# Cross-attention with a bit-weight feed-forward: the attention outputs leave in groups of eight heads instead of four

## The reference, cut to what matters

```python
x = x + xattn(layernorm(x), ctx, ctx)   # causal, softmax(q k^T / 8) v for each head
x = x + (layernorm(x) @ weight.T + bias)
# weight[o, i] = scale * sum_n (sigmoid(pweight) - sigmoid(nweight))[o, i, n] * exps[n] * sigmoid(mask)[n]
# bias[o] = rounded(clip(sum_n (pbias - nbias)[o, n] * bexps[n])) * biasscale
```

## Time and profile before

| | |
|---|---|
| median of 3 runs | 1179.91 us (1177.99 to 1181.48) |
| profiled execution, its own time | 1179.6 us |
| its span | 1177.8 us |
| mean granted TensorE clock | 0.987 |
| PE busy | 1099.1 us, 93% |
| DVE busy | 996.0 us, 85% |
| ACT busy | 855.9 us, 73% |
| POOL busy | 493.5 us, 42% |

### The profile page before, as it was taken

One profiled execution on the slowest core, in us unless ns is written; L12 is line 12 of the kernel. 1 busy time (PEld: TensorE's weight loads), 2 busy tenths in 40 slices (PEclk: granted clock), 3 DMA queues, 4 the chain that ended last, 5 costly groups with the idle time before them and its releaser, 6 DMA issues.

```text
span 1177.8 us, 32049 instructions
## 1 busy us (share of the span) xinstructions
PE 1099.1 (93%) x13092; PEld 809.3 (69%) x13092; DVE 996.0 (85%) x1558; ACT 855.9 (73%) x1764; POOL 493.5 (42%) x510
## 2 busy tenths in 40 slices
PE   4788988999999999999999999999999998999988
PEld 3677755676676777777776777777776676777753
DVE  5766788999988888999989888999989888998961
ACT  6789766778786677777876777878776777777740
POOL 3444424344236654343335655333335664331150
PEclk8899999999999999999999999999999999999989
DMA  9999726675669876656778886676678976664442
GB/s 320 321 322 351 242 73 138 148 160 113 140 121 202 200 169 143 141 140 135 134 132 201 195 162 134 133 153 140 116 149 202 189 169 121 133 119 86 89 84 72
DMA packets 382594, 191.13 MB, mean 162 GB/s; under 512 B 358128, under 2 KB 358128, under 8 KB 378352
## 3 DMA queue, kind: packets, MB, share of 16 engines
q1 hardware_dynamic: 381440, 189.05, 69.9%
q10 hardware_dynamic: 1008, 0.04, 0.1%
HBM read 67.15 MB, written 16.78 MB: 71 GB/s over the span
## 4 chain that ended last, share of the span: by engine, by line
PE 49%; DVE 19%; ACT 13%; DMA 8%; issue 6%; POOL 3%; SPq 2%; ACTq 0%; POOLq 0%; DVEq 0%
PE ffnb L473 16%; PE ptb L434 8%; PE slot L420 5%; PE slot L421 5%; DMA pd<-pd 5%; DVE pd L661 4%; DVE mx L647 4%; ACT p L542 4%; PE obank L454 4%; ACT pd L551 3%; ACT pt L558 3%; PE ffnb L497 3%; PE obank L457 3%; PE obank L455 3%; DVE stats L679 3%
## 5 line engine op out<-in xcount | busy, mean ns | idle before, releaser
L542 ACT ACTIVATE p<-slot,mx 128x512 f32<-128x512 f32 (+7 forms) x512 | 377.0, 744 | 137.2 <-issue 74.3
L647 DVE TENSOR_REDUCE mx<-slot 128x1 f32<-128x640 f32 (+7 forms) x352 | 356.1, 1014 | 31.7 <-PE slot L424 30.8
L473 PE MATMUL ffnb<-wt,yt 128*128 128x512 f16 x1464 | 372.4, 381 | 1.1 <-DMA yt<-y 0.8
L653 DVE SCALAR_TENSOR_TENSOR pt<-ptb,pt 128x512 f16<-128x512 f32 (+1 forms) x504 | 281.6, 598 | 51.4 <-ACT pt L558 49.9
L558 ACT ACTIVATE pt<-ptb 128x512 f16<-128x512 f32 (+1 forms) x504 | 239.8, 526 | 106.1 <-PE ptb L434 105.3
L420 PE MATMUL slot<-kt,qt 128*128 128x128 f16 (+3 forms) x1056 | 267.6, 283 | 7.1 <-DMA qs<-qt 2.5
L421 PE MATMUL slot<-kt,qs 128*128 128x128 f16 (+3 forms) x1056 | 267.6, 283 | 0.0
L883 POOL TENSOR_TENSOR ring<-ring,att 128x256 f32<-128x256 f32 x128 | 93.1, 727 | 393.1 <-DVE att L672 392.9
L434 PE MATMUL ptb<-id,p 128*128 128x128 f32 x1700 | 238.1, 278 | 10.8 <-DVE pt L653 10.6
L473 PEld LDWEIGHTS ffnb<-wt,yt 128*128 128x128 f16 x1464 | 137.3, 98 | 100.3 <-issue 2.5
L454 PE MATMUL obank<-v,pt 128*128 128x64 f16 x1700 | 176.4, 193 | 19.8 <-DVE att L672 12.2
(11 more groups left out here) (94 smaller groups left out, 1529.4 us busy)
## 6 DMA issues: line engine op xcount, KB each, us to landing
ring<-in_x_dram SPq DMA_DIRECT2D x32, 512.0 KB, 4.4
cin<-in_ctx_dram SPq DMA_DIRECT2D x32, 512.0 KB, 4.8
out_dram<-ring SPq DMA_DIRECT2D x32, 512.0 KB, 3.4
qs<-qt SPq DMA_DIRECT2D x124, 128.0 KB, 2.9
v<-in_weights_dram SPq DMA_DIRECT2D x11, 1024.0 KB, 8.7
kt<-in_weights_dram SPq DMA_DIRECT2D x11, 1024.0 KB, 8.0
pd<-in_weights_dram SPq DMA_DIRECT2D x5, 1024.0 KB, 8.0
yt<-in_weights_dram SPq DMA_DIRECT2D x5, 1024.0 KB, 8.6
```

Source lines behind the costliest of these rows:

```text
L473: last = pe.matmul(dst, yt[:, k % 2, a * KT_N + kk, :], wt[:, c, kk, half * 512:half * 512 + 512], start=r == 0, stop=r == 3 * KT_N - 1)
L542: last = nc.scalar.activation(p32[:, j.par, hh * j.keys:(hh + 1) * j.keys], slot[:, j.par, base:base + j.keys], ACT.Exp, bias=mx[:, j.par, ...
L647: nc.vector.tensor_reduce(mx[:, j.par, 0:j.heads], src[:, 0:j.heads, 0:j.keys], AX_X, ALU.max, negate=True).then_inc(mx_ready, 1)
L653: nc.vector.scalar_tensor_tensor(pt[:, j.par, j.blocks + blocks.start:j.blocks + blocks.stop, :], ptb[:, c % 2, 0:P * len(blocks)].rearran ...
```

## The change

`GROUP` goes from 4 to 8, so `GROUPS` goes from 4 to 2. The group's place becomes all 512 columns of `obank`; `att`, `rinv` and `mx` get eight heads. A tile then has two reciprocals, two scalings and two adds in place of four, each with twice the elements. In a 16-step tile a group opens at q = 0 and q = 8 and no longer at q = 4 and q = 12; in an 8-step tile at q = 0 and 4; in a 4-step tile at q = 0 and 2. The output of a group comes two iterations behind its last job. As a lot of the bias products takes the whole bank, the two lots are now made where no group is open: in iterations 5 and 7 instead of 4 and 5.

```diff
--- before.py
+++ after.py
@@ -24,7 +24,7 @@
 P_SCALE = 1024.0
 MASKED = -1e30
 ROUND = 1.5 * 2 ** 23
-GROUP = 4
+GROUP = 8
 GROUPS = H // GROUP
 
 
@@ -123,7 +123,7 @@
 LOADS = {4: (2, 2), 8: (4, 4), 16: (9, 9)}
 SWAP = {4: (0, 2), 8: (2, 6), 16: (6, 14)}
 
-BIAS_JOBS = (4, 5)
+BIAS_JOBS = (5, 7)
 BIAS = {4: 2, 8: 4, 16: 9}
 
 Y_LATE = {1: (6, 7, 7), TILES - 2: (12, 13, 14)}
@@ -252,7 +252,7 @@
         ffnb = stack.enter_context(nc.psum_tensor("ffnb", [P, 512], F32))
 
 
-        oacc = obank[:, 0:2, :].rearrange("p a b -> p (a b)").rearrange("p (h d) -> p h d", d=D)
+        oacc = obank[:, :, :].rearrange("p a b -> p (a b)").rearrange("p (h d) -> p h d", d=D)
 
         first_kt = slot[:, 0, :].bitcast(F16).rearrange("p (h c) -> p h c", c=P)
         first_qt = slot[:, 1, :].bitcast(F16).rearrange("p (h c) -> p h c", c=P)
@@ -439,7 +439,7 @@
                 if j.opens_group:
                     reached(pe, osb_done, j.group)
                 if j.n + 1 in BIAS_JOBS:
-                    pe.wait_ge(bias_out, j.n + 2 - BIAS_JOBS[0])
+                    pe.wait_ge(bias_out, BIAS_JOBS.index(j.n + 1) + 1)
                 if j.d is None:
                     pe.wait_ge(lo_done, j.chunks[-1][0] + 1)
                 else:
@@ -521,7 +521,7 @@
                 if j.n < UNITS:
                     weights(j.n)
                 if j.n in BIAS_JOBS:
-                    bias_part(j.n - BIAS_JOBS[0])
+                    bias_part(BIAS_JOBS.index(j.n))
                 for k, m0, m1 in matmuls_at(j.t, j.q):
                     linear(k, m0, m1)
             values(JOBS[-2])
@@ -621,7 +621,7 @@
                 if 0 <= j.n - 1 < UNITS:
                     weights_high(j.n - 1)
                 if j.n - 1 in BIAS_JOBS:
-                    bias_part(j.n - 1 - BIAS_JOBS[0])
+                    bias_part(BIAS_JOBS.index(j.n - 1))
                 high_parts(j)
                 if j.n + 1 < UNITS:
                     chunk_tanh(2 * j.n + 2)
```

## The result

The changed kernel takes 1192.44 us (median of five runs, 1187.01 to 1193.06) against 1179.91 us before: slower by 0.9%, ratio 1.0094, 95% interval 1.0072 to 1.0117. A second measurement gave 1.0103 (1.0085 to 1.0121). The profiled execution is the 1187.01 one, with a span of 1184.8 us, 7.0 us over the one before.

A forecast was written before the change was run, and what follows sets the result against it. PE, busy 93%, was taken as the bound. Tiles 4 to 31 (+10.9) and tile 3 (-1.3) gave +9.6, taken as +8.5 us on 1179.6: 1188 us, own range 1183 to 1192, range to be held 1177 to 1195.

The forecast's parts named there:

- The wait at q = 4 is no gain (0.14 us): Tiles i = t % 8 = 4 to 7: PE's 0.77 us wait goes, but scores at q = 9 leave only 0.14 us gain.
- Output ahead of q = 8, +0.27 us: All 16 tiles i = 4 to 7: the wider output makes PE wait 0.27 us longer each, 4.2 us together.
- L661 at q = 3, 0.51 us late in tile 13: Longer output and add delay GpSimd's L869 by 0.81 us; DVE's L661 ends 0.51 us later, 0.37 us reaching PE.
- a wait at q = 9 of 0.3 to 0.5 us in each tile: Sign: in each tile i = 4 to 7, PE's scores L420 newly wait 0.3 to 0.5 us on ScalarE's exponential L542.
- L661 at q = 12, 0.54 us longer for i = 5, 6, 7: GpSimd's L858 starts first and holds DVE's L661 0.54 us longer; cost taken as 0.55, 0.45 and 0.55 us.
- The turn at i = 4: At q = 12 L661 starts before L858 by 0.15 us, takes 0.82 not 2.42 us; PE waits of 0.84 us go.
- The sum: Batches 0 to 3 lose 2.0, 3.7, 3.5 and 1.7 us, together +10.9; with tile 3, +9.6, taken as +8.5 us.
- in tile 4 the order at q = 3: Tile 4, still disturbed by the start: the turn of order comes at q = 3; batch 0 is put at 2.0 us.
- Tile 3, foretold at -1.3: Tile 3 loses a 1.3 us wait on the output, a gain of that size.
- DVE paces: Faster rival: freed DVE time passes through, waits at q = 4 go (-8.6 us), giving 1174 us; chance 0.13.
- No collisions, about the same: Rival: the 512-wide add takes hardly longer, or DVE's delays at q = 3 and 12 are taken up; 1181 us, chance 0.16.
- The third rival: Slower: at i = 4 L858 keeps the port, four tiles lose 0.84 + 0.55 us each, +5.6, 1194 us; chance 0.16.

The follow-up runs named there:

- short add: Changed kernel, but GpSimd adds only four of a group's eight heads, leaving out half of the attention output: 1179.6 us, ratio 1.0002 to the kernel before.
- late add: Changed kernel, but in 16-step tiles GpSimd adds the group closed at q = 15 after the y split L869, not ahead of it: 1187.9 us, ratio 1.0079.
- both gates: GpSimd's y split waits for L661 of q = 3, its q split for L661 of q = 12: changed kernel 1174.1 us, kernel before 1173.3 us.
- the second profile: Profile from running the changed kernel again, unedited: median 1191.8 us, ratio 1.0103 to the kernel before; the profiled execution took 1192.8 us.
- the padded kernel: Kernel before plus a 256-element GpSimd add ahead of the y split and the bias add in 16-step tiles: 1186.7 us, ratio 1.0057.

## Why the prediction was right

*The wait at q = 4 is no gain (0.14 us).* Right. In tile 13 it was a slip of 0.77; with the short add, where nothing else differs at this place, the slip at q = 9 is 0.645. The gain is 0.13 us.

*Output ahead of q = 8, +0.27 us.* Right in kind, 0.30 us in tile 13 (slip 0.39 to 0.69). The reciprocal of eight is 193 ns and not 170, which is part of the 0.03.

*L661 at q = 3, 0.51 us late in tile 13.* It was 0.54 (1.50 against 0.96), in tile 15 0.70 (1.93 against 1.23; foretold 0.69). Of how this comes to PE I had the sum and not the places. I named only the scores of q = 9, with a wait of 0.3 to 0.5 us. In tile 13 PE slips 0.19 and 0.31 us in iteration 5, at the turned job's landing and at the transposes, and then the same 0.65 us at q = 9 as with no delay at all. The sum, 0.19 + 0.31 + 0.65 - 0.77 = 0.38, is the 0.37 foretold. Because I had it in one place, I expected the late add to free q = 9, and that was wrong. The sign "a wait at q = 9 of 0.3 to 0.5 us in each tile" came in 12 of the 16 tiles, with 0.10 to 0.57 us (0.43 to 0.57 in nine of them). It is missing in tiles 6, 23, 30 and 31; in 6 and 23 the delay shows as a longer wait for the landing of the turned job q = 3 (0.50 to 1.56 and 0.85 to 1.49 us). GpSimd's normalisation for the next q is earlier as foretold, by 4.1 us in tile 12 and 4.5 in tile 13.

*L661 at q = 12, 0.54 us longer for i = 5, 6, 7.* 0.55, 0.55 and 0.54 (2.70, 2.32, 2.04 against 2.15, 1.77, 1.50 us). The lock of the port, cited from the Trainium skill, page "SBUF — State Buffer", section "SBUF: two separate sides", says that whichever starts first keeps the port for its whole instruction, and the trace agrees for i = 5 to 7. How long the other stands I had from the earlier trace rows, not from the page, and that held to within 0.04 us there. For i = 4 at q = 3 L661 was 0.45 us late (1.28 against 0.83), 0.2 us less than the same reading gives.

*The turn at i = 4.* Right, by 0.08 us in tile 12 where I had 0.15.

*The sum.* +10.9 was foretold for tiles 4 to 31, and +11.1 measured. That they agree so closely is luck: a sum of tiles moves by 2 to 3 us from one profile to the next, and errors in three of the four batches cancel. Batch 1 is 3.6 (3.7 foretold). Batch 2 is 2.6 (3.5 foretold). Batch 0 is 4.7 with tiles 8 and 9 (+0.36 and +0.59, which I had at nothing) where I said 2.0: in tile 4 the order at q = 3 did not turn (L661 2.60 us), so that gain was not there. Batch 3 is -0.2 and not +1.7: tiles 28 and 30 became 1.2 and 0.8 us shorter, as waits for the landing of turned jobs shrank or went (1.24 to 0.53 us and 0.43 to nothing in tile 28, 1.12 to nothing in tile 30). That is no accident of one profile. Tile 30 is 44.3 to 44.7 us long in all four profiles with groups of four, and 43.3 to 43.7 in all six with groups of eight. It is a gain of the change that I did not foresee, and no run shows how it comes about. Tile 3, foretold at -1.3, gave -0.05; when its wait on the output went, waits on transposes and on the linear half took its place (values 1.46 to 0.41 us, transposes 1.50 to 2.02, linear 0.97 to 1.47).

*The rivals.* "DVE paces" is refuted: with both gates, groups of eight and four are level, and before that the kernel became slower and not faster. "No collisions, about the same" (1181) is what the short add makes of the kernel: 1179.6. The third rival did not come about in either profile of the changed kernel, though it was only 0.08 us away.

*From 1188 to 1192.4.* The median lies 4.4 us above the forecast, just outside the forecast's own range of 1183 to 1192 and inside the range to be held. The first profile, 1187.0, agrees with 1188 partly by luck. From the 1179.6 of the profile of before, tiles 4 to 31 add 11.1 us, what follows them takes off 1.7, the start up to the end of tile 3 takes off 2.3, and the device time exceeds the span by 0.4 us more. The start is not an effect of the change: it is 174.8 to 178.3 us long with groups of four and 175.0 to 178.1 with groups of eight. The shorter end may be one, and I had it at nothing: the stretch behind tile 31 is 38.8 to 40.4 us in the six profiles with groups of eight and 40.5 to 41.9 in the four with groups of four. Between the first two profiles, 0.6 us of it is the wait for the last turned job (2.67 to 2.05 us), and 1.1 us the first 48 matmuls behind it, which began at a granted clock of 0.68 before (1140.7 to 1147.0 us) and 0.86 after (1148.8 to 1155.0 us).

Without its short start the first profile would be at about 1189.4. The other 3 us of the median lie in the start and in stretches like tile 24's, as far as the second profile shows. Why the padded kernel has a median 5 us below is open: its profiled execution, 1186.7, and the first one of the changed kernel, 1187.0, agree within 0.3 us in the start, in the tiles and in what follows, and the difference is in executions that were not profiled.

## What to carry to other kernels

A longer GpSimd instruction cost nothing for itself here, on an engine that is 42% busy, but it moved all that was queued behind it, and where that meets a VectorE instruction with two SBUF inputs, the one that starts second stands until the other is done, as L661 did behind L858 (2.70 us in place of 0.96). Before joining two small instructions into one, list for each such meeting who comes first and by how much. Where GpSimd has room, let it wait for VectorE: two such waits made the kernel before 0.7% faster. And a wait of the busiest engine is worth only the distance to the next thing that is late, 0.14 us of 0.77 here.

## What was unexpected of the hardware

The order at the port follows the start times down to 0.05 us: 474.52 against 474.57 went to GpSimd, 473.28 against 473.36 to VectorE. The GpSimd split that lost took 2.73 in place of 2.13 us, so the waiting shows as duration on both engines. This is a good part of why VectorE's busy time did not fall (996.0 and 996.3 us) while 128 instructions and 19 us of outputs went; with the short add, which takes the longer holds away, it is 980.1 us.

The same kernel took 2.6 us longer in one tile in one execution than in another: 0.9 us in a wait for a DMA, and 1.6 at the lower clock that followed it.
